# Moving the vector engine's marking list and the overflow test in a graph, linear-attention and expert-routing block

## The reference

```
h1  = relu(segment_sum((xn @ W1.T + b1)[src], dst))        # graph layer 1
h2  = relu(segment_sum((h1 @ W2.T + b2)[src], dst))        # graph layer 2
q   = softmax(xn @ Wq.T, rows) * 512**-0.5 ; k = softmax(xn @ Wk.T, columns) ; v = xn @ Wv.T
mix = q @ (k.T @ v) + xn ;  mix = mix @ M1.T @ M2.T + xn
x   = x + h2 + mix
out = x + experts(layernorm(x))      # Sinkhorn gates, top 156 rows for each of 8 experts
```

## Time and profile before

| | us |
|---|---|
| median of 3 runs | 503.98 |
| lowest and highest | 503.56, 504.63 |
| the profiled execution | 503.98 |
| its span in the profile | 501.4 |
| around the span (the difference) | 2.6 |
| PE busy | 476.1 (95%) |
| DVE busy | 330.8 (66%) |
| ACT busy | 139.1 (28%) |
| POOL busy | 71.4 (14%) |

### The profile page before, as it was taken

How to read it: one execution, slowest core, us unless ns; L and a number is a source line. 1 busy time by engine, 2 the same in 40 slices (tenths; PEclk the granted TensorE clock), 3 DMA queues, 4 the chain that set the end, 5 groups by cost and what they waited for, 6 DMA issues and landing times.

```text
span 501.4 us, 6890 instructions
## 1 busy us (share of the span) xinstructions
PE 476.1 (95%) x2475; PEld 379.1 (76%) x2475; DVE 330.8 (66%) x1121; ACT 139.1 (28%) x245; POOL 71.4 (14%) x94
## 2 busy tenths in 40 slices
PE   7879999999999999999999999999999988789995
PEld 3667788888888888887799998778888656566663
DVE  6893689798998988895631104445545566767772
ACT  5455463322333232341231102221231360001110
POOL 3476010000000000000040000010000000056652
PEclk9999999999999999999999999999999679999999
DMA  8800202011000000003000000055444860054541
GB/s 228 242 1 2 83 1 85 1 47 59 1 2 0 2 0 1 2 1 118 1 3 2 1 1 1 0 164 192 126 136 141 307 226 1 1 133 135 143 123 48
DMA packets 18012, 34.60 MB, mean 69 GB/s; under 512 B 2939, under 2 KB 3269, under 8 KB 17972
## 3 DMA queue, kind: packets, MB, share of 16 engines
q1 hardware_dynamic: 15156, 26.82, 16.7%
q0 software_dynamic: 2816, 7.26, 5.3%
HBM read 24.25 MB, written 10.24 MB: 69 GB/s over the span
## 4 chain that ended last, share of the span: by engine, by line
PE 85%; DVE 9%; issue 2%; DMA 1%; SPq 1%; ACT 1%; POOLq 0%; DVEq 0%
PE ps L632 46%; PE ps L893 8%; PE ps L845 8%; PE ps L736 5%; PE ps L619 4%; PE ps L910 3%; PE ps L938 2%; PE ps L878 1%; DMA X<-in_x 1%; PE ps L975 1%; PE ps L768 1%; DVE XF L1226 1%; PE ps L872 1%; DVE MASK L1619 1%; PE ps L929 1%
## 5 line engine op out<-in xcount | busy, mean ns | idle before, releaser
L1432 DVE TENSOR_SCALAR RING_D<-places,PLACES 125x170 bf16<-125x170 f16 (+1 forms) x239 | 62.0, 259 | 0.0
L1433 DVE TENSOR_SCALAR RING_S<-iota,HOME 125x128 bf16<-125x128 f16 x239 | 58.9, 246 | 0.0
L845 PE MATMUL ps<-AT,H1H 125*128 125x416 f32 (+1 forms) x108 | 38.0, 352 | 0.0
L845 PE MATMUL ps<-AT,H1L 125*128 125x416 f32 (+1 forms) x108 | 38.0, 351 | 0.0
L893 PE MATMUL ps<-H2H,AT 125*125 125x512 f32 x90 | 36.2, 402 | 0.0
L910 PE MATMUL ps<-WE0H 128*128 128x512 f32 x106 | 35.7, 470 | 0.0
L893 PE MATMUL ps<-H2L,AT 125*125 125x512 f32 x90 | 35.5, 394 | 0.0
L580 POOL DMA_INDIRECT YX<-scratch,idx x16 | 17.1, 1068 | 113.4 <-DVE idx L1681 108.8
L1498 DVE TENSOR_TENSOR ps<-ps,bias 125x512 f32<-125x512 f32 x20 | 14.0, 699 | 28.0 <-PE ps L632 28.0
L530 POOL TENSOR_TENSOR G2L<-RAW_G,G2H 128x512 fp32r<-128x512 f32 x4 | 5.0, 1286 | 192.0 <-ACT G2H L994 192.0
L1577 DVE SCALAR_TENSOR_TENSOR ZL<-ps,ZH 128x416 fp32r<-128x416 f32 (+1 forms) x12 | 6.3, 584 | 38.7 <-ACT ZH L1137 38.7
(11 more groups left out here) (350 smaller groups left out, 1246.6 us busy)
## 6 DMA issues: line engine op xcount, KB each, us to landing
RAW_E<-in_experts SPq DMA_DIRECT2D x8, 1024.0 KB, 10.1
out_x<-X SPq DMA_DIRECT2D x10, 224.0 KB
scratch<-X SPq DMA_DIRECT2D x10, 224.0 KB
scratch<-Y SPq DMA_DIRECT2D x10, 224.0 KB
X<-in_x SPq DMA_DIRECT2D x4, 448.0 KB
RAW_K<-in_WkT SPq DMA_DIRECT2D x4, 256.0 KB, 4.2
RAW<-in_mW2T SPq DMA_DIRECT2D x1, 1024.0 KB, 11.9
RAW_A<-in_mW SPq DMA_DIRECT2D x1, 1024.0 KB, 14.0
```

Source lines behind the costliest of these rows:

```text
L845: pe.matmul(place(f), h[0:TT, k, 128 * f:128 * (f + 1)], AT[0:TT, k, c0:c1], start=(k == 0 and n == 0), stop=False)
L1432: V.tensor_scalar(hot_d(v, width(b)), places[0:ET, 0:width(b)], PLACES[0:ET, c:c + 1], None, ALU.is_equal)
L1433: V.tensor_scalar(hot_s(v), iota[0:ET, :], HOME[0:ET, c:c + 1], None, ALU.is_equal).then_inc(done["marked"], 1)
```

## The change

Five edits:

1. The flag's matmul moves from the context stage to the z stage, in front of the third product of the first chunk, and becomes two matmuls that add up: `over`, as before, and `many`, which is 1 where the source rows of one partition have more than 4096 edges together. `many` comes from `odeg`, a sum that ACT's copy of each group now also writes (`accum_out`), and two small DVE instructions. DVE's read of the flag moves from the head of its list to behind the last `h1_left`.
2. PE's register load and the branch to `count_again` move from ahead of z into the first residual branch (after 72 matmuls of the first chunk). On its taken side `count_again` is now written out group by group, and 72 matmuls of the chunk are done again.
3. DVE's hand-written order changes: `value_left(0)` and `value_scale()` come ahead of the entry (vp1, 6), and from there on every piece of other work stands one entry earlier in the list. 18 entries instead of 19 are marked when the loop over the tiles begins; the lines of that loop are the same.
4. ACT splits g2 after the fourth h tile (i == 3), not after the tenth.
5. Inside `count_again`, two PSUM banks in turn and exact widths.

```
-    use("flag", (7,), ("flag_ready", 1))            # psum_plan, behind "keys"
+            if ch == 0 and f == 2:                    # psum_plan, in the z loop
+                use("flag", (7,), ("flag_ready", 1))
@@ PE
-                if i == NT - 2:
-                    pe.wait_ge(done["flag_in"], 1)
-                    closes("flag", pe.matmul(opens("flag")[0:1, 0:1], over[0:TP, 0:1], ones[0:TP, 0:1], start=True, stop=True))
...
-                with pe.Fori(0, NG) as g:
-                    pe.wait_ge(done["again_go"], g + 1)
+                for g in range(NG):
+                    if g >= 2:
+                        pe.wait_ge(done["again_read"], g - 1)
                     tiles_again(g, 0, True)
...
-            pe.wait_ge(done["adj_hi"], NG)
-            pe.wait_ge(done["flag_ready"], 1)
-            large.append(pe.value_load(flag[0:1, 0:1], min_val=0, max_val=1))
-            with pe.If(large[0] > 0):
-                count_again()
-            with pe.Else():
-                pe.nop()
...
+                    if ch == 0 and f == 0:
+                        pe.wait_ge(done["adj_hi"], NG)
+                    if ch == 0 and f == 2:
+                        pe.wait_ge(done["flag_in"], 1)
+                        flag_ps = opens("flag")[0:1, 0:1]
+                        pe.matmul(flag_ps, many[0:TT, 1:2], ones[0:TT, 0:1], start=True, stop=False)
+                        closes("flag", pe.matmul(flag_ps, over[0:TP, 0:1], ones[0:TP, 0:1], start=False, stop=True))
+                    gather_rows(f, ch == 0 and f == 0)
                 if ch == 0:
                     pe.wait_ge(done["h1l_ready"], NT)
+                    pe.wait_ge(done["flag_ready"], 1)
+                    large.append(pe.value_load(flag[0:1, 0:1], min_val=0, max_val=1))
                 with pe.If(large[0] > 0):
+                    if ch == 0:
+                        count_again()
+                        for f in range(C):
+                            gather_rows(f, again=True)
@@ ACT
-                nc.scalar.activation(AT[0:TT, :, lo:hi], counts_of(g), ACT.Copy).then_inc(done["adj_hi"], 1)
+                nc.scalar.activation(AT[0:TT, :, lo:hi], counts_of(g), ACT.Copy, accum_out=odeg[0:TT, g:g + 1]).then_inc(done["adj_hi"], 1)
...
-            for c in range(C):
-                split_hi("g2", c)
+                if i == 3:
+                    for c in range(C):
+                        split_hi("g2", c)
@@ DVE
-            reads(dve, "flag")
-            V.tensor_scalar(flag[0:1, 0:1], ps_of("flag")[0:1, 0:1], 0.5, None, ALU.is_gt).then_inc(done["flag_ready"], 1)
             mark_next()
             total_left(0)
             total_left(1)
             total_left(2)
             mark_next()
             total_left(3)
+            value_left(0)
+            value_scale()
             mark_next()
-            for c in range(C):
-                value_left(c)
-                if c == 0:
-                    value_scale()
+            split_lo("wq", 0)
+            mark_next()
+            value_left(1)
+            mark_next()
+            split_lo("wq", 1)
+            mark_next()
+            value_left(2)
+            mark_next()
+            split_lo("wq", 2)
+            mark_next()
+            value_left(3)
+            mark_next()
+            split_lo("wq", 3)
+            for c in range(1, C):
                 mark_next()
-                split_lo("wq", c)
+                context_left(c - 1)
                 mark_next()
-            for c in range(C):
-                context_left(c)
-                mark_next(2)
+            mark_next()
+            context_left(C - 1)
+            mark_next(2)
...
+            after("adj_hi", NG)
+            link(V.tensor_reduce(many[0:TT, 0:1], odeg[0:TT], AX, ALU.add))
+            V.tensor_scalar(many[0:TT, 1:2], many[0:TT, 0:1], EXACT, None, ALU.is_gt).then_inc(done["flag_in"], 1)
+            reads(dve, "flag")
+            V.tensor_scalar(flag[0:1, 0:1], ps_of("flag")[0:1, 0:1], 0.5, None, ALU.is_gt).then_inc(done["flag_ready"], 1)
             after("flag_ready", 1)
             large = dve.value_load(flag[0:1, 0:1], min_val=0, max_val=1)
```

More of the change, by code:

```diff
@@ L318, in gps_block @@
         krs = small("krs", [128, 2, C], F32, "a")
+        odeg = small("odeg", [128, NG], F32, "a")
+        many = small("many", [128, 2], F32, "a")
         flag = small("flag", [128, 1], I32, "a")
@@ L822, in count_again @@
                         tiles_again(g, n, False)
-                    pe.matmul(ps[:, 0:2], zero[0:1, 0:TT], zero[0:1, 0:2], start=False, stop=True,
+                    pe.matmul(PS[4 + g % 2][0:TT, 0:2], zero[0:1, 0:TT], zero[0:1, 0:2], start=False, stop=True,
                               skip_group_check=True).then_inc(done["again_full"], 1)
-                pe.wait_ge(done["again_go"], NG + 1)
-            pe.wait_ge(done["adj_hi"], NG)
-            pe.wait_ge(done["flag_ready"], 1)
-            large.append(pe.value_load(flag[0:1, 0:1], min_val=0, max_val=1))
-            with pe.If(large[0] > 0):
-                count_again()
-            with pe.Else():
-                pe.nop()
+                pe.wait_ge(done["again_read"], NG)
             for ch, (c0, c1) in enumerate(CHUNKS):
@@ L837, in place, with gather_rows @@
                     return PS[plan[f"z{ch}_{f}"][0]][:, 0:c1 - c0]
+                def gather_rows(f, fresh=False, again=False):
+                    for k in range(NT - 1):
+                        if fresh:
+                            pe.wait_ge(done["h1l_ready"], k + 1)
+                        for n, h in enumerate((H1H, H1L)):
+                            pe.matmul(place(f), h[0:TT, k, 128 * f:128 * (f + 1)], AT[0:TT, k, c0:c1], start=(k == 0 and n == 0), stop=False,
+                                      skip_group_check=again)
                 for f in range(C):
                     opens(f"z{ch}_{f}")
[L841 to L845, removed]
+                    if ch == 0 and f == 0:
[6 more added lines that the diff above has]
+                    gather_rows(f, ch == 0 and f == 0)
                 if ch == 0:
                     pe.wait_ge(done["h1l_ready"], NT)
+                    pe.wait_ge(done["flag_ready"], 1)
+                    large.append(pe.value_load(flag[0:1, 0:1], min_val=0, max_val=1))
                 with pe.If(large[0] > 0):
+                    if ch == 0:
+                        count_again()
+                        for f in range(C):
+                            gather_rows(f, again=True)
                     for k in range(NT):
@@ L1335, in tiles_left @@
                 link(V.tensor_tensor(left[0:TP], left[0:TP], touch[0:TP], ALU.mult))
-                V.tensor_reduce(over[0:TP, 0:1], left[0:TP].rearrange("p h b -> p (h b)"), AX, ALU.add).then_inc(done["flag_in"], 1)
+                V.tensor_reduce(over[0:TP, 0:1], left[0:TP].rearrange("p h b -> p (h b)"), AX, ALU.add)
             def chosen_keys():
@@ L1552, in count_again @@
                     d = slice(lo, hi)
-                    ps = PS[4][0:TT, 0:NT * (hi - lo)].rearrange("p (d k) -> p k d", k=NT)
-                    link_again(V.tensor_copy(AT[0:TT, :, d], ps))
-                    V.tensor_tensor(AL[0:TT, :, d], ps, AT[0:TT, :, d].bitcast(F32), ALU.subtract).then_inc(done["again_go"], 1)
-                after("again_go", NG + 1)
+                    link_again(V.tensor_copy(AT[0:TT, :, d], counts_of(g)))
+                    V.tensor_tensor(AL[0:TT, :, d], counts_of(g), AT[0:TT, :, d].bitcast(F32), ALU.subtract).then_inc(done["again_read"], 1)
+                after("again_read", NG)
             def residual(first, c0, c1):
                 with dve.If(large > 0):
+                    if first == 0:
+                        count_again()
                     for k in range(NT):
@@ L1567, in residual @@
                     dve.nop()
-            with dve.If(large > 0):
-                count_again()
-            with dve.Else():
-                dve.nop()
             for ch, (c0, c1) in enumerate(CHUNKS):
```

12 lines of the change are left out of this document (6 added, 6 removed).

## The result

The changed kernel takes 528.22 us (median of 4 runs, 527.36 to 532.12), the kernel before beside it 503.77 (4 runs): a ratio of 1.049, with an interval of 1.045 to 1.054. The forecast was 521.0 in a range of 516.5 to 527.0. The direction was right; the time lies above the range.

A forecast was written before the change was run, and what follows sets the result against it. PE alone was taken to set the end from about 62 to 387 us, so only added PE work or PE waits count. 503.98 + 14.8 (order) + 2.0 (g2's split) + 0.2 (flag) = 521.0 us, range 516.5 to 527.

The forecast's parts named there:

- The branch: In z: one taken branch less on PE and DVE, one register load moved; taken as 0.
- The rival: In z's first chunk, PE stalls on up to three instruction fetches of 1.05 us: 3.2 us, 524.2 in all; 7 in 100.
- DVE's order: From vp1 to the h stage, marks written one entry later make PE wait at its visits: 14.8 us.
- closed circle: Each loss runs product end, ACT copy, DVE rest, DVE marks, PE; it recurs with every product, earlier waits not helping.
- g2's split: In h4 and h5, POOL's four instructions now run beside DVE's marks and hold them: 2.0 us, between 0 and 5.0.
- The flag: On PE, one f32 matmul in two passes goes and two come: +0.2 us net, between 0 and 0.5.
- ACT's sums: 0.19 us more in each of 25 copies: taken as 0, bound 4.8; rival that they hold the banks, 525.8, 3 in 100.
- The clock: Granted clock falls in PE's new waits: up to 529.8 us, or 523.9 for a fall a third as long; 5 in 100.
- the signs named ahead: Profile after: PE's visits carry idle time ended by DVE's line 1433; PE idle from 95 to 275 us sums to 15 to 20.
- some 17: Sign in the profile after: z begins some 17 us later.
- Everything behind it keeps its length: Sign in the profile after: all that follows z's later start keeps its length.
- the sign for the branch: In z: if the first matmuls of line 859 have idle time, the branch rival holds.

The follow-up runs named there:

- compact_moved: `branch_only` with `count_again` back in its short form of two nested loops; 503.16 us, ratio 0.9985.
- long490: `compact_moved` with 80 more matmuls (160 instructions) on the never-taken side of the branch; 505.79 us, ratio 1.004.
- repaired: The kernel after with DVE's old list and the short `count_again` in loops, all other parts kept; 503.99 us, ratio 0.9986.
- order_only: The kernel before with DVE's new order alone; 522.06 us, ratio 1.037.
- branch_only: The kernel before with the branch part alone: `count_again` written out and the branch moved behind 72 matmuls of z's first chunk; 510.10 us, ratio 1.013.

## Why the prediction was wrong

**The step that failed is "The branch": "I take 0".** It costs 5.5 us in z's first chunk (5.8 less the flag's 0.36), of which 3.9 are idle time, and 1.4 of lower clock in the other two. The rival had the mechanism and 3.2 of these. The reason given against it was that no row behind the branches of before shows idle time. That evidence was beside the question: each of them jumps over some 170 instructions, so it lands in the piece that is fetched ahead anyway. The Trainium skill ("Runtime: NRT & Kernel Launch", "Instruction fetch mechanics") sets the condition, a target outside the two pages present, and the prediction itself noted that by it "the new branch would, the old ones might not". The silence of the old ones is what the rule says of them, and was counted against it. `compact_moved` against `long490` now shows the rule at work, with 0 against 0.82 us of idle time. With 3.2 for the branch the forecast would have been 524.2. The rival's price was three packets of 1.05 us each. The runs show two, and none if the landing lies in the next piece; but PE goes on only 2.4 to 2.9 us after a packet starts, and then at the lower clock.

**DVE's order, 14.8: right mechanism, 16.3 measured.** From the starts of the visits, per product, predicted and measured: vp1 0.2 and 0.28; vp2, vp3, cp0 0.76 and 0.85; cp1 to q0 0.91 and 1.06, 1.06, 0.98, 0.92; q1 1.3 and 1.37; x0 to x8 nothing and nothing; x9 1.35 and 1.40; h 6.0 and 6.7. The number of waits was right: one per product, in front of matmul 6, and 0.01 or less at matmul 0. What was too small is the price of each. In vp2 the third visit starts 0.78 late, as reckoned (0.76), but the matmul behind it starts 0.08 after it and not 0.02, as behind a visit that didn't wait. That is 0.06 per wait, 1 us for the 17. In h the reckoned 0.98 came as 1.0 to 1.1 (h2 to h6). The claim that each wait is a closed circle that recurs with every product holds.

**g2's split, 2.0: 1.5 measured, plus 0.8 of lower clock** in the one execution that had it. The 2.0 was taken between 0 and 5.0 without a working, and it came close because POOL catches few marks (one in h4 of the kernel after) and only what the lead doesn't cover counts; with the lead intact three caught halves of marks cost 0.41.

**The flag, +0.2: +0.36 in z and -0.32 in the context stage.** From start to start in the earlier trace rows, the matmul and the one behind it had cost 0.21 + 0.11. The sum is nothing.

**ACT's sums, 0: 0.** `repaired` has all 25 of them.

**The clock, a rival with 5 in 100:** its share is 2.2 us outside z's first chunk and at most 1.5 in it (5.5 less the 3.9 of idle time), far from the 8.8 of its upper end. It should have been no rival but a possible part of the price of other waits: it came behind both gaps of the jump each time, behind POOL's wait in one of two traces, and behind none of the 17 waits of `order_only`.

Of the signs named ahead, the waits stand in the products that were named, but not as idle time of PE's visits: PE is idle for 6.7 us between 95 and 275, not 15 to 20. Each row's duration runs on past the next start, and so counts as busy what the starts show as waiting. z began 17.1 later ("some 17"), which is luck in part: the stretches ahead of it lost 18.6, and the head was 1.4 shorter. A mark beside POOL took over 0.3. "Everything behind it keeps its length" did not, and the sign for the branch stood in the tail's rows and not in z's first ones, since the branch stands there.

## What to carry to other kernels

The size of code that never runs is a cost on an engine that streams its instructions: keep the rare side of a branch in loops, short enough that the jump lands in the next 16 KB, or expect one to two fetches of 2.4 to 2.9 us each, of which PE was idle for 0.8 to 1.3 (the first) and 2.0 to 3.0 (the second). Where there were two, the lower clock came behind them. A producer's lead over the engine that bounds the kernel is a stock: an entry taken away once is paid at most later meetings (17 waits here, none in x0 to x8, which had time to spare), and one entry put back, tried at one point, ended it from there on. When a rule has a condition, evidence from cases outside the condition says nothing against it.

## What the hardware showed that was not expected

- After a jump to code that isn't there, PE waited a second time (2.0 to 3.0 us) two to four matmuls on in seven kernels, though the first fetch had taken 2.4 us or more in which the next piece could have come. Its packet starts only 0.6 to 1.1 us after PE has gone on (269.46 and 270.07 in `branch_only`, 288.29 and 289.43 in the kernel after).
- By the packets, no-operations in the source are not in the program (24 instruction packets with and without 400 of them, at the same distances to 0.7 us; 25 and a gap of 0.80 with 200 matmuls).
- 3.05 us of idle PE at one go left the granted clock full in the one profile taken; behind two gaps of together 3.0 to 3.9 us it fell in all seven, and behind one of 1.06 us, after shorter waits in the tiles before, in one trace of two.
